# Filler matmuls between the units of the first attention

## The reference

```python
x = x + xattn(layernorm(x), ctx, ctx, Wi, bi, Wf, bf, ln_scale)
#   per head: C = (q k^T / sqrt(dh)) * D,  D = exp(log_D - max), lower triangle
#   h = (C / max(|sum C|, exp(-max))) v, normalised per head, times ln_scale
x = x + ffn(layernorm(x), gate_up (fp4 + group scales), down (fp4 + group scales))
#   h = silu(gate) * up;  y = h W_down;  y / rms(y)
```

## Time and profile before

| | us |
|---|---|
| median of 3 runs | 647.42 (647.1 to 650.89) |
| the profiled execution | 646.62 |
| its span, first to last instruction | 644.6 |
| PE busy in the span | 546.7 (85%) |
| VectorE busy | 453.5 (70%) |
| ScalarE busy | 298.9 (46%) |
| POOL busy | 317.2 (49%) |
| mean granted PE clock | 0.891 |

### The profile page before, as it was taken

The page is one execution under the profiler, slowest core; times in us unless marked ns, Lnnn a source line. Parts: engine busy times, 40 slices in busy tenths (PEclk is TensorE's granted clock), DMA queues, the critical chain, the costliest instruction groups (busy, mean ns, idle before and its releaser), DMA issues.

```text
span 644.6 us, 7996 instructions
## 1 busy us (share of the span) xinstructions
PE 546.7 (85%) x2638; PEld 316.9 (49%) x2638; DVE 453.5 (70%) x741; ACT 298.9 (46%) x646; POOL 317.2 (49%) x341
## 2 busy tenths in 40 slices
PE   3628999827999995998999995979999969877997
PEld 3227889414666543444666444336666434322342
DVE  4877774994888798545888896536888873688601
ACT  3164435425777701355776513346777201655300
POOL 2213332542677665204776861235776840488700
PEclk9855558866999998898999996998999998999999
DMA  8044120106410300036102100064100001200000
GB/s 216 12 123 156 51 66 14 54 0 198 164 33 2 132 1 1 33 124 237 66 2 89 42 1 1 33 216 166 46 2 2 1 0 50 82 1 0 1 33 33
DMA packets 20883, 39.96 MB, mean 62 GB/s; under 512 B 7275, under 2 KB 7915, under 8 KB 20331
## 3 DMA queue, kind: packets, MB, share of 16 engines
q1 hardware_dynamic: 20842, 39.46, 18.2%
HBM read 30.93 MB, written 4.33 MB: 55 GB/s over the span
## 4 chain that ended last, share of the span: by engine, by line
PE 49%; DVE 28%; issue 8%; ACT 5%; POOL 4%; DMA 2%; SPq 2%; DVEq 0%; POOLq 0%; ACTq 0%
PE pf L893 14%; PE po L835 9%; PE pf L905 8%; PE pq L803 7%; POOL ffn L497 3%; DVE tok L1144 3%; DVE bst L1003 2%; DVE ffn L1182 2%; PE pq L765 2%; PE pq L815 2%; DVE ffn L1178 2%; ACT th L637 2%; DVE hT L1222 2%; PE pq L840 2%; DVE tok L1158 2%
## 5 line engine op out<-in xcount | busy, mean ns | idle before, releaser
L905 PE MATMUL pf<-w_down,hT 128*128 128x512 f32 x352 | 154.3, 596 | 0.0
L497 POOL TENSOR_TENSOR ffn<-ffn,ts 128x512 f32<-128x512 f32 x88 | 111.8, 1271 | 69.9 <-DVE ffn L1182 62.5
L893 PE MATMUL pf<-yT,gu_val 128*128 128x512 f16 x544 | 136.8, 390 | 10.9 <-DVE ffn L1178 7.6
L630 ACT ACTIVATE ts<-pf,gu_scale 128x512 f32<-128x512 f32 x136 | 86.4, 686 | 59.6 <-PE pf L893 59.2
L905 PEld LDWEIGHTS pf<-w_down,hT 128*128 128x128 f32 x352 | 66.5, 191 | 83.6 <-issue 78.0
L459 POOL TENSOR_SCALAR_AFFINE_SELECT dmat<-dmat 128x512 f32<-128x512 f32 x64 | 43.3, 679 | 89.9 <-ACT dmat L596 89.8
L893 PEld LDWEIGHTS pf<-yT,gu_val 128*128 128x128 f16 x544 | 48.7, 99 | 78.1 <-DVE ffn L1182 15.5
L596 ACT ACTIVATE dmat<-negm,aT 128x128 f32<-128x128 f32 x256 | 80.2, 395 | 8.2 <-DMA negm<-negm_dram 8.2
L835 PEld LDWEIGHTS po<-v_sb,dmat 128*128 128x128 f32 x512 | 70.5, 215 | 5.3 <-issue 1.7
L835 PE MATMUL po<-v_sb,dmat 128*128 128x33 f32 x512 | 69.4, 294 | 0.0
L502 POOL TENSOR_TENSOR hT<-ffn,th 128x512 f32<-128x512 f32 x44 | 64.5, 1468 | 0.0
(11 more groups left out here) (120 smaller groups left out, 744.2 us busy)
## 6 DMA issues: line engine op xcount, KB each, us to landing
negm<-negm_dram SPq DMA_DIRECT2D x32, 512.0 KB, 5.2
ffn<-in_x SPq DMA_DIRECT2D x4, 1024.0 KB, 6.5
ctx_sb<-in_ctx SPq DMA_DIRECT2D x4, 1024.0 KB, 5.4
x_sb<-in_x SPq DMA_DIRECT2D x4, 1024.0 KB, 5.4
x_res<-x_sb SPq DMA_DIRECT2D x4, 1024.0 KB, 4.8
out<-x_res SPq DMA_DIRECT2D x16, 256.0 KB, 2.0
x_res<-in_L_ffn_gate_up_packed SPq DMA_DIRECT2D x1, 704.0 KB, 6.0
th<-in_L_ffn_down_packed SPq DMA_DIRECT2D x1, 352.0 KB, 6.6
```

Source lines behind the costliest of these rows:

```text
L497: pool.tensor_tensor(acc, acc, ts[:, h % TDEEP, 1], ALU.add).then_inc(tsum_ready, 1)
L630: act.activation(ts[:, h % TDEEP, g], bank(q, h, g), ACT.Copy, scale=gu_scale[:, g * GU + o:g * GU + o + 1]).then_inc(t_ready, 1)
L893: last = pe.matmul(bank(q, h, g), gu_val[:, h // 2 + h % 2 * FT, g], yT[:, part, g], start=(part == 0), stop=(part == 1))
L905: last = pe.matmul(pf[:, tt], hT[:, j, tt * P:(tt + 1) * P], w_down[:, j], start=(j == 0), stop=(j == FT - 1))
```

## The change

A function `keep_busy(count)` issues that many matmuls of the f16 identity, with the identity four times over as moving operand (512 columns), into bank 3 of `pf`. Nothing reads them. It is called with 14 ahead of the first `iteration`, and with 7 behind each `state_sums` in the first `iteration`, that is seven times. To have bank 3 free, the weight preparation takes turns over three banks instead of four; its waits are adapted, in PE's and in ScalarE's list.

```diff
                 for n in GU_PREP.get(j, ()):
                     act.wait_ge(gut_done, n + 1)
                     act.activation(gu_val[:, 2 * n:2 * n + 2].rearrange("q o g k -> q (o g k)"),
-                                   pf[:, n % 4].bitcast(F16), ACT.Copy, scale=FP4_SCALE).then_inc(gut_read, 1)
+                                   pf[:, n % 3].bitcast(F16), ACT.Copy, scale=FP4_SCALE).then_inc(gut_read, 1)
                 for n in DN_PREP.get(j, ()):
                     act.wait_ge(dnt_done, n + 1)
-                    act.activation(w_down[:, n], pf[:, n % 4], ACT.Copy).then_inc(dnt_read, 1)
+                    act.activation(w_down[:, n], pf[:, n % 3], ACT.Copy).then_inc(dnt_read, 1)
...
-                    if n >= 4:
-                        pe.wait_ge(gut_read, n - 3)
+                    if n >= 3:
+                        pe.wait_ge(gut_read, n - 2)
...
-                                pf[:, n % 4].bitcast(F16)[:, k:k + P],
+                                pf[:, n % 3].bitcast(F16)[:, k:k + P],
...
-                    if n >= 4:
-                        pe.wait_ge(dnt_read, n - 3)
+                    if n >= 3:
+                        pe.wait_ge(dnt_read, n - 2)
...
-                            pf[:, n % 4, o * P:(o + 1) * P],
+                            pf[:, n % 3, o * P:(o + 1) * P],
...
+            def keep_busy(count):
+
+                for _ in range(count):
+                    pe.matmul(pf[:, 3], ident16[:], ident16[:].unsqueeze(1).to_broadcast([P, 4, P]),
+                              start=True, stop=True)
...
                             if q is None and VALUES[h] + 1 < UNITS:
                                 scores(p, q, VALUES[h] + 1, 1)
                                 state_sums(p, q, VALUES[h] + 1)
+                                keep_busy(7)
...
             turn_back(0)
+            keep_busy(14)
             iteration(0, None, 1)
```

## The result

The changed kernel takes 654.94 us (median of six executions, 650.09 to 655.55), the kernel before beside it 647.71 us. The ratio of the two is 1.0092, with a 95% interval of 1.0057 to 1.0128: slower by about 6 us. The profiled execution took 655.07 us with a span of 653.0, 8.45 us over the profiled one of before. So the sign is settled, and the size lies between 1 and 8 us. The forecast was 648.0 us, with a range from 641.0 to 653.0.

A forecast was written before the change was run, and what follows sets the result against it. PE at half clock was taken to bound the first attention, VectorE next. A held clock gave -5.8 us, lost units +4.4 and +2.8, so +1.4 on the profiled 646.62: 648.0 us, range 641.0 to 653.0.

The forecast's parts named there:

- near 75: First attention, after unit 2's scores and values: the raised clock falls again while PE waits 1.5 us for VectorE.
- rival A: First attention: clock won in unit 1, lost for one to three of units 2 to 5; 643.8 to 651, chance 0.6.
- The term of the sum: First attention, units 3 and 4 at half clock: +4.4 and +2.8 us lost again.
- unchanged, so the gain passes whole: Behind the first attention: VectorE's normalisation chain stays unchanged, so the held-clock gain of 5.8 us reaches the total.
- I am wrong if the later stages change their length by themselves: Stages behind the first attention: all should shift alike; a change of their own length would refute the forecast; no size given.
- B: First attention: the clock, once risen, is held at full; -5.8 us, 640.8, chance 0.17.
- that schedule: First attention with the clock held full from about 65 us: values of the last unit end at 109.2, total -5.8 us.
- C: Units 2 to 5: clock lost early, won back late, four units or more at half speed; 653 to 655, chance 0.1.
- E: First attention: clock holds, but VectorE sets every unit's pace at 7.4 to 7.65 us; -4 us, 642.6, chance 0.07.
- D: First attention: fillers don't lift the clock, or busy time alone counts; about 17 us slower, 663.6, chance 0.06.

The follow-up runs named there:

- e1: Changed kernel without any filler matmuls, only the three banks: 647.90 us, ratio 0.9992 to the kernel before.
- e2: Changed kernel without the groups of seven, keeping three banks and the 14 fillers ahead of the loop: 649.90 us, ratio 1.0014 to the kernel before.
- e0_again: The changed kernel run again, unedited, on another occasion: 652.76 us, ratio 1.0046 to the kernel before.
- e9_split: Changed kernel with each seven replaced by four fillers ahead of the values and four ahead of the state sums: 647.29 us, ratio 0.9962 to the kernel before.
- the better placings: e9_split without the 14 or the last unit's four before state sums, six added after unit 0's scores: 643.42 us; with POOL waiting for both halves of squares, 640.78.
- e6: Changed kernel, but POOL scales the first attention's heads only when both halves of the squares are there: 647.76 us, ratio 1.0007 to the kernel before.

## Why the prediction was right and wrong

The forecast was 648.0, the median 654.94 and the profiled execution 655.07.

*Right, by its steps.* PE bound the stretch, and busy PE did not lift the clock. Seven fillers cost 3.0 us at half clock and 1.5 at full: 2.99 and 1.51. The 14 and the ring of three banks cost nothing (e1, e2). The clock rose near 65 and fell in the narrow work of unit 2 or 3: 64.6 and 78.3, against "near 75". Values 2, 3 and 4 were put at 74.8, 85.95 and 96.15 us and ended at 75.1, 85.5 and 95.7. The products of units 2 and 3 were put at 69.25 and 76.9, and came at 69.60 and 77.08. The trace is a case of rival A with three lost units, for which I had +4.5 at the end of the attention; it was +3.9. That the values came out to within half a microsecond is partly luck: in e0_again values 2, 3 and 4 ended at 77.1, 82.5 and 92.8.

*Wrong, first: how long the clock stays lost.* I counted two units, with the clock back "at the latest" in unit 5, and gave unit 5 its full-clock price of 7.1 us. It took 10.3, since the clock came back at 102.2, after its seven fillers and about half of its transposes. The term of the sum was +7.2 us for lost units, and measured about +10. Rival A also put one lost unit at about 3 us, where its own working has +4.4 for the first. In e0_again the same term was about +5: the last addition ended at 115.9, against 110.5 for a held clock. So the size of this term changes from execution to execution, and one number for it was too little.

*Wrong, second: "unchanged, so the gain passes whole".* VectorE's chain behind the attention is not a fixed block. Its first instructions met POOL's, +2.6 us, in both traces of the changed kernel. In the kernel before they just miss each other. I had looked at what VectorE waits for at the seam, and not at what runs beside it; the same four instructions at 4.7 us in the later iterations of the trace of before would have told it.

*Wrong, third: "I am wrong if the later stages change their length by themselves".* They did, by 1.9 us here and 4.3 in e0_again. I named it and gave it no room in the range, which ended at 653.0. What cost the 4.3 us stays open but for the last 1.6.

The rivals: B, the clock held, needed another placing of the same fillers (e9_split), and even then the values of unit 7 ended 3.1 us earlier than before, not the 4.7 of that schedule, with eight fillers a unit, four of them ahead of the rise at 66.5, and unit 0 later by 1.4. C had the number, 653 to 655, for four lost units or more; three were lost in one trace, and the rest came from behind the attention. E, VectorE setting the pace, came true only in the better placings, in units 2 to 4. D fell: the clock rose in every kernel with fillers beside the state sums. The Trainium skill, TensorE: Matmul & The Clock Gate, Part 1, says that sustained PE activity opens the gate. The traces agree only if busy PE of the profile isn't that activity: 23.7 us busy of 23.7 at 0.50 here.

## What to carry to other kernels

Where filler matmuls stand decides whether they pay: in one block behind the narrow work they lost 5 us at the end of values 7 in one trace and 1 in another, and nearly as many in two blocks around it gained 3. Count a filler at its half-clock price until a trace shows that it pays, and put it where the engine waits anyway. Take a second trace before a size is read from the first. When a stage is moved by some microseconds, look at what runs beside the short instructions at its end, on the other engine too.

## What the runs showed of the hardware that was not expected

- VectorE instructions of 0.2 to 0.3 us took 1.07 to 1.33 us beside POOL instructions of 1.2 to 1.5 us (three in the first attention of the changed kernel, four in each later iteration of the kernel before), each as if it had to wait for one to end; a 2.29 us reduction took the same beside them (e6) and alone (the changed kernel, POOL idle from 123.7).
- 28 matmuls of 128x32 f16 with the same stationary identity took 0.80 us at half clock, 0.03 us each.
- The same program ran with its half-clock stretches in other units in other executions (78.3 to 102.2 in one trace of the changed kernel, 83.5 to 90 and 94 to 96.5 in another), and the executions of the kernel before spread over 8 us, the longer ones at the lower mean clock (0.897 to 0.882).
